# A gated cross-attention layer: the value product in fp16, and a new order inside each step of the attention loop

## The reference

```python
x = x + tanh(g_xattn[0]) * xattn(_layernorm(x), ctx, ctx, Wq, Wk, Wv, Wo, bo, mask)
# in xattn, 16 heads of 64:
qh, kh, vh = split_heads(q @ Wq), split_heads(k @ Wk), split_heads(v @ Wv)
dots = einsum('bhid,bhjd->bhij', qh, kh) * SCALE    # masked, causal
attn = softmax(dots)
out  = einsum('bhij,bhjd->bhid', attn, vh)          # "pv" below
return out.reshape(b, n, h * d) @ Wo + bo
```

## Time and profile before

| | |
|---|---|
| median of 3 runs | 1624.89 us |
| the profiled execution's own time | 1626.47 us |
| its span (first to last instruction) | 1624.6 us |
| TensorE busy in the span | 94% |
| VectorE | 85% |
| ScalarE | 77% |
| GpSimd | 64% (none in the last part) |

### The profile page before, as it was taken

One profiled execution on the slowest core, in us unless ns is written; L12 is line 12 of the kernel. 1 busy time (PEld: TensorE's weight loads), 2 busy tenths in 40 slices (PEclk: granted clock), 3 DMA queues, 4 the chain that ended last, 5 costly groups with the idle time before them and its releaser, 6 DMA issues. The chain is left out here.

```text
span 1624.6 us, 38058 instructions
## 1 busy us (share of the span) xinstructions
PE 1530.6 (94%) x12556; PEld 1251.8 (77%) x12556; DVE 1385.1 (85%) x2247; ACT 1253.4 (77%) x3222; POOL 1033.8 (64%) x1004
## 2 busy tenths in 40 slices
PE   7899999999999999999999999789989997995998
PEld 5787887877877878878778788677767776775887
DVE  7888888888888888888888889878887998998996
ACT  5887887888778778878887787566758998885674
POOL 3988988888888889888888888600006664740000
PEclk9999999999999999999999999999998999997999
DMA  6554445444444544454444445369957884755664
GB/s 195 118 127 103 105 106 122 104 92 115 106 105 103 126 102 105 107 121 104 92 115 106 105 103 98 86 205 344 321 215 262 282 287 153 276 227 187 218 214 145
DMA packets 347365, 252.23 MB, mean 155 GB/s; under 512 B 287792, under 2 KB 317616, under 8 KB 344368
## 3 DMA queue, kind: packets, MB, share of 16 engines
q1 hardware_dynamic: 347312, 251.58, 55.1%
HBM read 105.25 MB, written 76.02 MB: 112 GB/s over the span
## 5 line engine op out<-in xcount | busy, mean ns | idle before, releaser
L496 ACT ACTIVATE prob<-masked,neg_max 128x128 f32<-128x128 f32 x1024 | 397.6, 391 | 35.1 <-DVE neg_max L662 31.6
L431 POOL TENSOR_TENSOR prob_parts<-prob,prob_parts 128x512 f16<-128x512 f32 x254 | 310.3, 1241 | 2.7 <-ACT prob_parts L504 1.6
L426 POOL TENSOR_TENSOR prob<-prob,scaled 128x512 f32<-128x512 f32 x256 | 271.6, 1061 | 20.1
L660 DVE TENSOR_TENSOR masked<-score,mask_add 128x512 f32<-128x512 f32 x256 | 174.6, 682 | 74.0 <-PE score L963 67.9
L504 ACT ACTIVATE prob_parts<-prob 128x512 f16<-128x512 f32 x254 | 159.0, 627 | 75.6 <-POOL prob L426 71.7
L496 ACT ACTIVATION_READ_ACCUMULATOR prob<-masked,neg_max 128x1 f32 x1024 | 193.3, 189 | 0.0
L662 DVE TENSOR_REDUCE neg_max<-masked 128x4 f32<-128x512 f32 x256 | 175.6, 686 | 8.8
L438 POOL TENSOR_TENSOR probT<-turn 128x512 f32<-128x512 f16 x125 | 173.2, 1386 | 0.0
L1723 POOL TENSOR_SCALAR xThi<-n_x 128x1024 fp32r<-128x1024 int16 x15 | 43.8, 2919 | 202.9 <-DMA n_x<-n_x_d 166.8
L976 PE MATMUL y<-wo_hi,o_hi 128*128 128x256 f32 x508 | 148.3, 292 | 15.9 <-DVE o_lo L667 15.2
L424 POOL TENSOR_TENSOR scaled<-rsums,pscale 128x4 f32<-128x4 f32 x256 | 66.4, 259 | 124.0 <-DVE rsums L654 123.9
(11 more groups left out here) (249 smaller groups left out, 4485.5 us busy)
## 6 DMA issues: line engine op xcount, KB each, us to landing
gate<-gate_d SPq DMA_DIRECT2D x30, 768.0 KB, 4.3
n_x<-n_x_d SPq DMA_DIRECT2D x25, 512.0 KB, 4.9
gate_d<-stage SPq DMA_DIRECT2D x8, 1536.0 KB, 5.5
n_u_d<-w_raw SPq DMA_DIRECT2D x16, 768.0 KB, 4.1
stage<-n_u_d SPq DMA_DIRECT2D x16, 768.0 KB, 6.0
gate_d<-gate SPq DMA_DIRECT2D x7, 1536.0 KB, 5.5
x_in<-in_x SPq DMA_DIRECT2D x16, 512.0 KB, 3.9
ctx_in<-in_ctx_columns SPq DMA_DIRECT2D x16, 512.0 KB, 4.8
```

The source lines that it names most:

```text
L426: gp.tensor_tensor(prob[:, h], prob[:, h], scaled[:, h, :].rearrange("p (b o) -> p b o", o=1).broadcast_to([P, NB, P]), ALU.mult).then_inc ...
L431: gp.tensor_tensor(prob_parts[:, h, 1], prob[:, h].rearrange("p b k -> p (b k)"), prob_parts[:, h, 0], ALU.subtract).then_inc(prob_low, 1)
L496: nc.scalar.activation(prob[:, h, b, :], masked[:, h, b, :], ACT.Exp, bias=neg_max[:, h, b:b + 1], accum_out=psums[:, h, b:b + 1]).then_in ...
L660: nc.vector.tensor_tensor(masked[:, h], score[h][:], mask_add[:], ALU.add).then_inc(masked_done, 1)
```

## The change

v is held in fp16, as a high and a low part (`v16`), scaled so that it can't overflow: the scale of a group comes from a bound, the product of the largest context values and the largest Wv values, which TensorE forms with two one-column passes (`value_bound`). The scale is taken back in the residual (`y_unit`). pv uses the transposed fp16 halves in `turn` themselves: high x high, high x low and low x high, 24 passes of 128 columns in fp16 for 16 in fp32; `probT` and both joins are gone, and SyncE's transpose waits for pv itself before it writes `turn` again. For every v job ScalarE writes the high part and after it VectorE the low part. In a step of TensorE the v jobs come ahead of the output product, and the scores ahead of pv. GpSimd's bias addition moves from c = 6 to c = 0 of the next group. In the first steps ScalarE's weight splits stand in another order.

```diff
-        v_sb = sb("v_sb", [P, NB, INNER])
+        v16 = sb("v16", [P, NB, 2, 2, VH], F16)
@@ turn_prob (SyncE)
-                wait(sp, probT_copied[h], u - 1)
+                wait(sp, pv_done, u - 1)
@@ step (GpSimd)
-                if old:
-                    join_second(u - 3, (c + 1) % 2, NC // 2 * g + (c - 1) // 2)
-                if c == 6 and new:
-                    gp.wait_ge(xres_loaded, 16 * (g + 1))
-                    gp.tensor_tensor(xres[:], xres[:], bo_g[:].rearrange("p (o n) -> p o n", o=1).broadcast_to([P, NB, D]),
-                                     ALU.add).then_inc(xres_ready, 1)
+                if c == 0 and not (isinstance(g, int) and g == 0):
+                    add_bias(g - 1)
+                if c == 6 and new and not more:
+                    add_bias(g)
@@ ScalarE
+            def values_high(g, i, n):
+                b, before = nth(g, i)
+                if n == 0:
+                    act.wait_ge(v_scaled, 4 * g + 3)
+                act.wait_ge(projected[b], before + 1)
+                nc.scalar.activation(v16[:, n % NB, n // NB, 0], proj[b][:], ACT.Copy, scale=v_mul[:, 0:1]).then_inc(v_high, 1)
@@ step (ScalarE)
                 if soft:
                     exps(u - 1, 0)
-                if new:
+                if new and not early:
                     copy_k(g, c, u)
+                for i, n in vs[:1]:
+                    values_high(g, i, n)
...
                 if soft:
                     exps(u - 1, 1)
...
-                if new and c > 2:
-                    for i, n in jobs_of(c, "v"):
-                        b, before = nth(g, i)
-                        act.wait_ge(projected[b], before + 1)
-                        nc.scalar.activation(v_sb[:, n % NB, VH:2 * VH], proj[b][:], ACT.Copy).then_inc(copied[b], 1)
+                for i, n in vs[1:]:
+                    values_high(g, i, n)
@@ VectorE
-            def join_prob(u, h, slot, times):
...
+            def values(g, jobs):
+                for i, n in jobs:
                     b, before = nth(g, i)
+                    dve.wait_ge(v_high, NC * g + n + 1)
+                    nc.vector.scalar_tensor_tensor(v16[:, n % NB, n // NB, 1], proj[b][:], v_mul[:, 0:1], v16[:, n % NB, n // NB, 0],
+                                                   ALU.mult, ALU.subtract).then_inc(copied[b], 1)
+            def ctx_top(g):
+                dve.wait_ge(ctx_loaded, 16 * (g + 1))
+                nc.vector.tensor_reduce(c_top[:], ctx_in[:], X, ALU.max, apply_absolute_value=True).then_inc(v_scaled, 1)
@@ step (VectorE)
-                if old:
-                    join_prob(u - 3, 0, (c + 1) % 2, NC // 2 * g + (c - 1) // 2)
+                if c == 4:
+                    output_unit(g)
+                if c == 6 and more:
+                    ctx_top(g + 1)
...
+                if isinstance(g, int) and u == 0:
+                    value_scale(0)
+                vs = jobs_of(c, "v")
+                if new:
+                    values(g, vs[:1])
                 if soft:
                     reciprocals(u - 1, 1)
-                if c < 3:
-                    values(g, c)
+                if new:
+                    values(g, vs[1:])
+                if nxt:
+                    value_scale(g + 1)
@@ VectorE, before the loop
+            dve.wait_ge(w_loaded[5], 16)
+            nc.vector.tensor_reduce(w_top[:], w_stage(2), X, ALU.max, apply_absolute_value=True)
+            ctx_top(0)
             w_low_part(3)
@@ times_v (TensorE)
-                    pe.wait_ge(probT_copied[h], u + 1)
+                        pe.wait_ge(prob_turned[h][slot], 16 * times)
...
-                    for h in range(2):
-                        last = nc.tensor.matmul(pv[h * HD:(h + 1) * HD, b, :], v_sb[:, b, c * P + h * HD:c * P + (h + 1) * HD],
-                                                probT[:, h, b, :], start=True, stop=True)
+                    for n, (m, t) in enumerate(((0, 0), (0, 1), (1, 0))):
+                        for h in range(2):
+                            at = c % NB * P + h * HD
+                            last = nc.tensor.matmul(pv[h * HD:(h + 1) * HD, b, :], v16[:, b, c // NB, m, at:at + HD],
+                                                    turn[:, slot, h, t * NB + b, :], start=(n == 0), stop=(n == 2))
@@ step (TensorE)
+                if first:
+                    value_bound(0)
                 if nxt:
                     transpose_in(g, *ts[0])
+                if new:
+                    for i, n in jobs_of(c, "v"):
+                        value(g, i, n)
                 if oldest:
...
                     out_product(u - 4, (c - 4) % NC)
                 if nxt:
                     transpose_in(g, *ts[1])
+                    value_bound(g + 1)
                 if new:
-                    for i, n in jobs_of(c, "v"):
-                        value(g, i, n)
-                if old:
-                    times_v(u - 3, co, (g, c, u) if new else None)
-                if new:
-                    if not old:
-                        scores_free(g, c, u)
-                    scores(g, c, u)
+                    scores_free(g, c, u)
+                    pe.nop(nofuse=True)
+                    scores(g, c, u)
+                if old:
+                    times_v(u - 3, co, (c + 1) % 2, NC // 2 * g + (c - 1) // 2)
```

More of the change, by code:

```diff
@@ L202, in attention @@
         xres_loaded = sem("xres_loaded")
-        probT_copied = [sem(f"probT_copied{h}") for h in range(2)]
+        v_high = sem("v_high")
+        v_scaled = sem("v_scaled")
+        v_bound = sem("v_bound")
+        last_turned = sem("last_turned")
         pv_done = sem("pv_done")
@@ L573, in _ @@
             attended(U - 2)
-            act.wait_ge(last_step, 1)
             act.wait_ge(pv_done, U - 1)
-            nc.scalar.activation(probT[:, 0], trans[:], ACT.Copy).then_inc(probT_copied[0], 1)
-            for n in range(4):
+            for h in range(2):
+                act.wait_ge(last_step, h + 1)
+                nc.scalar.activation(turn[:, 1, h, 0:NB], trans[:], ACT.Copy).then_inc(v_high, 1)
+                if h == 0:
+                    ffn_high_part(0)
+            for n in range(1, 4):
                 ffn_high_part(n)
@@ L642, in w_low_half @@
                     last.then_inc(w_ready, 1)
-            def join_prob(u, h, slot, times):
-                dve.wait_ge(prob_turned[h][slot], 16 * times)
-                wait(dve, pv_done, u)
-                nc.vector.tensor_tensor(probT[:, h], turn[:, slot, h, 0:NB], turn[:, slot, h, NB:2 * NB],
-                                        ALU.add).then_inc(probT_copied[h], 1)
             def reciprocals(u, h):
@@ L679, in make_mask, with value_scale, output_unit @@
                 dve.wait_ge(mask_ready, g + 1)
-            def values(g, c):
-                for i, n in jobs_of(c, "v"):
+            def values(g, jobs):
+                for i, n in jobs:
                     b, before = nth(g, i)
-                    dve.wait_ge(projected[b], before + 1)
-                    nc.vector.tensor_copy(v_sb[:, n % NB, 0:VH], proj[b][:]).then_inc(copied[b], 1)
+                    dve.wait_ge(v_high, NC * g + n + 1)
[4 more added lines that the diff above has]
+                nc.vector.tensor_reduce(c_top[:], ctx_in[:], X, ALU.max, apply_absolute_value=True).then_inc(v_scaled, 1)
+            def value_scale(g):
+                dve.wait_ge(v_bound, g + 1)
+                nc.vector.tensor_scalar(v_unit[:], trans[:, 0, 0:1], 1.0 / VMAX, VTINY, ALU.mult, ALU.max).then_inc(v_scaled, 1)
+                dve.wait_ge(v_scaled, 4 * g + 2)
+                nc.vector.reciprocal(v_mul[:], v_unit[:]).then_inc(v_scaled, 1)
+            def output_unit(g):
+                if isinstance(g, int) and g == 0:
+                    dve.wait_ge(bo_ready, 2)
+                nc.vector.tensor_tensor(y_unit[:], tg_small[:], v_unit[:], ALU.mult).then_inc(v_scaled, 1)
             def step(g, c):
@@ L821, in _ @@
             for h in range(2):
-                nc.vector.memset(score[h][:], 0.0).then_inc(score_zero, 1)
+                nc.vector.memset(score[h][:], 0.0)
             w_low_part(0)
@@ L847, in _ @@
             attended_low(U - 3)
-            for h in range(2):
-                join_prob(U - 2, h, 0, U // 2)
             attended_low(U - 2)
             weight_values(2, 1)
-            ffn_low_part(0)
-            dve.wait_ge(last_step, 2)
-            dve.wait_ge(pv_done, U - 1)
-            nc.vector.tensor_copy(probT[:, 1], trans[:]).then_inc(probT_copied[1], 1)
+            for h in range(2):
+                dve.wait_ge(v_high, NC * G + h + 1)
+                nc.vector.tensor_tensor(turn[:, 1, h, NB:2 * NB], trans[:], turn[:, 1, h, 0:NB], ALU.subtract).then_inc(last_turned, 1)
+                if h == 0:
+                    ffn_low_part(0)
             for n in range(1, 4):
```

75 lines of the change are left out of this document (45 added, 30 removed).

## The result

The changed kernel takes 1654.7 us (median of four runs, 1654.1 to 1655.0) where the kernel before takes 1624.5 (1623.0 to 1626.1): a ratio of 1.0185, 95% interval 1.0168 to 1.0203. It is slower, as forecast, but by 30 us where 11.5 were forecast: inside the full range of 1606 to 1672, and above rival A's own range, which ended at 1650.

The account below looks back on a forecast made before the run. TensorE, busy 62.8 of 63.8 us a group, was taken to bound the kernel. +6.5 us for 15 groups (+0.43 each), +4 at the start and +1 at the end made 1624.9 + 11.5, some 1636 us; range 1606 to 1672.

Parts of the forecast that it names:

- rival A: The forecast itself: the fp16 block is short, but waits for copies eat the gain; 1636 us, 1625 to 1650, chance 0.47.
- the sum of the group: All eight TensorE steps of a group added up: 64.27 us against 63.84 before, +0.43 a group.
- all high: Every forecast stall at the upper end of its 0 to 0.4 us uncertainty: 64.6 us a group, +11 us.
- c = 7: Step where VectorE ends 1.4 to 2.1 us in and kT is done near 5.7: 8.25 us, before 7.83.
- c = 5: Step with late moments, maxima near 2.3 us and kT 0.1 late for the scores: 7.55 us, before 7.94.
- the term for the start: First v waits for the maxima over Wv and the context, starting at some 19.7 us: +4 us (2 to 6).
- The fp16 block: TensorE's pv with 24 fp16 passes: 0.83 us instead of 1.03, -0.20 a step, -1.6 a group.
- Rival C: Slower, as fp16 pairs are paced by their loads or dispatch: pv 1.15 us, 1676 us, chance 0.13.
- v against qT and kT: TensorE's earlier v waits for ScalarE's qT and kT copies: c = 4 8.07 us, c = 0 10.34 us.
- rival B: Faster, as freed ScalarE and VectorE run early enough to keep v's waits short: 1609 us, chance 0.35.
- VectorE's load: VectorE's work after joins and copies go and low halves and context maximum come: net -3.0 us a group.
- D: Gains and waits cancel over the whole kernel: 1625 us, chance 0.05.

Follow-up runs that it names:

- by the maximum: Changed kernel with VectorE's maximum over the next contexts in c = 6 cut to 16 of 512 columns from the second group on: 1646.4 us (1.0107).
- by the moments: Changed kernel with residual late, context maximum in c = 3, v of c = 0 behind the output product, and second LayerNorm's moments directly behind its statistics: 1612.1 us.
- the fastest kernel: Changed kernel with residual late, context maximum in c = 3, v of c = 0 behind the output product, second LayerNorm's moments early: 1612.1 us (0.9907).

## Why the prediction's direction was right, and where its sizes were wrong

The step that failed is the sum of the group, 64.27 us, where 65.20 was measured (above the 64.6 that "all high" gave): its terms for c = 7 and c = 5 took VectorE's operations at their durations of before, and left the output product's wait for o_lo out. The second is the term for the start, 4 us, which took TensorE's clock at its level of before. The mechanism of the other terms held.

**The fp16 block: right.** 0.79 us where 0.83 was taken. Rival C, and with it the 1.12 of the rule I had weighed, are out: 12 pairs in 0.79 us are at most 0.066 a pair, with the tile shape's change still inside it. The Trainium skill ("TensorE: Matmul & The Clock Gate", Back-to-back issue gap) has 81 ns a matmul for a stream of load and matmul at 128 columns. Taken per pair of column tiles, as I had taken it, the trace disagrees, and the measurement decides; what one such stream over the whole array takes, no run here shows.

**v against qT and kT: right.** v of c = 4 at 3.40 (3.50 forecast), residual at 5.99 (6.06), c = 0 10.38 (10.34) with both waits, plain steps 7.34 (7.43), c = 4 7.98 (8.07). Moving the residual, and v in c = 0, gave back these stalls. By this alone rival B was out: freed time on ScalarE, GpSimd and VectorE didn't move qT's copy up in its queue.

**c = 7: the wrong wait, and mis-sized by 0.96 us a group, 14 us in all.** The forecast had VectorE end 1.4 to 2.1 us into c = 7; it ended at 3.11. The normalise operations started 1.2 us later against the step than before (forecast 0.4 to 1.1), and I gave them their duration of before, though two of the four now run beside GpSimd's product and low part: 2.93 us instead of 2.09. And I let only the transposes wait for them; the output product's o_lo stands in the same queue behind them, and that wait, 1.19 us, is the larger. That VectorE's queue is the cause is shown by the edits that take work out of it: 9.21 to 8.81 by the maximum, and to 8.55 by the moments. That the normalise is longer because of GpSimd is read from the traces; no edit moved it alone. It fits that in the kernel before with only TensorE's order changed two of the four are long as well (1.30 and 1.12, one beside the bias addition), 2.98 in all, and c = 7 grew there too.

**VectorE's load: mis-sized, -0.5 us a group where -3.0 was forecast.** The operations taken out and put in cost what they were given. But the mask, the normalise and the second LayerNorm's moments, which the change doesn't touch, took some 1.8 us more in all, for they now meet GpSimd's operations at other points; the longest mask operation took 1.94 us where the longest before took 1.12. GpSimd's bias addition, moved to c = 0, is what lies there now.

**c = 5: mis-sized, 0.48 us a group, 7 us.** The forecast had the moments "late" and the maxima at 2.3, which is where they were (454.10 is 2.38 into the step), but took it that this cost only 0.1, and that the output product no longer waited for o_lo. In VectorE's queue o_lo stands behind the first maxima, and on ScalarE kT's copy behind the exponentials that need them: the output product started 4.43 us into c = 5 (4.22 in c = 3), the scores 6.40 (5.72), and c = 5 took 8.03 instead of 7.55. With the residual moved it is 7.65, with the moments early 7.34. The gain in the other steps (4 x 0.09 and 0.19 in c = 6, less 0.04 in c = 0) paid back 0.5 us a group.

**The start: mis-sized, 7.5 us instead of 4.** VectorE there in the kernel after, then TensorE:

```profile
15.72 2.29 DVE L872 TENSOR_REDUCE w_top<-v 128x2 f32<-128x2048 f32 x1 [1.24 <-DMA v<-in_L_xattn_Wv]
17.93 1.21 DVE L702 TENSOR_REDUCE c_top<-ctx_in 128x2 f32<-128x1024 f32 x1
```

```profile
19.19 1.01 PE L1002 MATMUL trans<-w_top,c_top 128*128 128x1 f32 x4 [4.67 <-DVE c_top L702]
...
25.64 0.50 PE L927 MATMUL proj<-tx_hi,wq_hi 128*128 128x512 f32 x1
```

Two stretches of the start in the kernel after, then the same two in the kernel before (columns as in the earlier trace rows; the third number from the end is the granted clock):

```profile
17.00:24.00 7.00, 4.81 (x13) 3.99 (x14) 5.27 (x8) 0.93 (x2) 0.57 (x2) 0.51 0.23 58
44.50:51.30 6.80, 5.53 (x40) 3.62 (x40) 4.53 (x8) 4.26 (x15) 6.64 (x7) 0.50 0.65 170
```

```profile
17.00:24.00 7.00, 6.46 (x55) 4.86 (x56) 4.78 (x7) 2.77 (x4) 1.30 (x2) 1.00 0.85 272
44.50:51.30 6.80, 5.91 (x32) 4.57 (x32) 6.53 (x11) 5.53 (x18) 6.18 (x8) 1.00 0.39 74
```

The two maxima are as forecast (2.29 and 1.21; the piece landed at 15.7, forecast 15.9). The first v started at 20.06, forecast 19.7. But step 1 started at 25.64, not 24.5: 4.7 late, not 3.5, for behind TensorE's wait of 4.67 us the passes of v stood 0.43 us apart and not 0.23. The other 2.9 us come in the first group's later steps, most of it in c = 3, which takes 11.98 us (before 9.38). Its waits are nearly the same, 1.76 us for v's low half and 1.27 for qT, together 3.03 (before 2.8); its passes again stand 0.43 apart. From these distances I estimate the price of the lower clock at some 4 us of the 7.5. The forecast put this term at nothing. What makes the clock fall there was not tested; the kernel before with only the order changed has neither.

The sum of the misses: 15 x 0.93 (65.20 less 64.27) is 14, and 3.5 at the start, 17.5 us, about the 18 between the forecast's 1636 and 1654.7. The end was +1.2 where +1 was forecast.

Rivals B and D asked for a group no longer than before; it is 1.36 us longer. What stays open: c = 7 is still 8.55 us in the fastest kernel (its output product waits 0.98 for o_lo; the four normalise operations there still take 2.93 us, but no edit tests them), what keeps c = 6 and 7 long with v in its old place, and why a wait of 1.93 us on TensorE is followed by a lower granted clock in some groups and, in others, only the next long wait is.

## What to carry to other kernels

When a block is moved on the bounding engine, move its copies on the other queues with it, and for every instruction that now waits, list what stands behind it in that queue: the price is the lateness of the last of these, not of the first. The order of two products on the bounding engine has to be weighed step by step: v ahead of the output product gained 0.33 us in c = 5 of the kernel before and lost 0.87 in c = 0, where the queue that copies its operands has extra work. And when GpSimd is freed of work, what it still does moves in time, and meets other operations of VectorE than before. On VectorE, put small operations where GpSimd idles, ahead of the instruction that releases GpSimd, and not behind it.

## What the runs showed of the hardware

The LayerNorm's operations of VectorE on four columns take 1.03 to 1.14 us instead of 0.16 when they start while GpSimd's product or low part runs, and end with it; the normalise on 256 columns takes up to 1.257 instead of 0.382. Not every operation is hit. One that reads the scores from PSUM keeps its time beside GpSimd (masked 0.68 at 470.36, inside GpSimd's 469.07 to 471.45), and so do the reciprocal of four columns (0.17 to 0.18 in each such case) and the maximum over 1024 columns (1.19 and 1.21). The Trainium skill ("SBUF — State Buffer", Who interferes with whom) tells of a port that VectorE and GpSimd share and that one of them can hold; the trace agrees, and it adds the price, some 1 us for an operation that itself takes 0.16.

Sixteen fp32 and twenty-four fp16 passes of 128 columns, two heads side by side, took 1.03 and 0.79 us, three halves of the passes in three quarters of the time. And a wait of TensorE of 1.93 us within otherwise full work was followed by a lower granted clock in ten of fourteen groups (0.85 over the whole step of 11.10 us), and in the other four the clock fell behind the wait for o_lo in c = 7; the step in which it fell was 1.4 to 1.6 us longer than the same step without.
